# A new transition from the token stage to the attention groups in a one-core transformer block

## The reference, cut to what matters

```python
Q, K, V = heads(xn @ wq.T + bq), heads(xn @ wk.T + bk), heads(xn @ wv.T + bv)   # 16 heads of 32
Q, K = elu(Q) + 1, elu(K) + 1
KV    = einsum('bhsd,bhse->bhde', K, V)        # one 32x32 matrix per batch and head
K_sum = sum(K over tokens)
att   = (Q @ KV) / (Q @ K_sum + 1e-8)          # per token and head
attention = att @ wo.T + bo
# ffn: 8 experts' LoRA pairs (rank 8), the top 2 of a router, beside a shared LoRA pair
w = top2 weights of sigmoid(xn @ W_router) + bias
gate, up = (xn @ W + shared LoRA + weighted expert LoRA) for W in (W_gate, W_up)   # 1376 columns
ffn = (silu(gate) * up) @ W_down + shared LoRA + weighted expert LoRA
```

## Time and profile before

| | |
|---|---|
| median of 3 runs | 704.85 us |
| the profiled execution, its own time | 704.41 us |
| its span (first to last instruction) | 702.6 us |
| PE busy | 675.8 us (96%) |
| DVE busy | 388.3 us (55%) |
| ACT busy | 252.7 us (36%) |
| POOL busy | 125.3 us (18%) |
| mean granted TensorE clock | 0.992 |

### The profile page before, as it was taken

How to read it: one execution, slowest core, us unless ns; L and a number is a source line. 1 busy time by engine, 2 the same in 40 slices (tenths; PEclk the granted TensorE clock), 3 DMA queues, 4 the chain that set the end, 5 groups by cost and what they waited for, 6 DMA issues and landing times.

```text
span 702.6 us, 10690 instructions
## 1 busy us (share of the span) xinstructions
PE 675.8 (96%) x3636; PEld 553.8 (79%) x3636; DVE 388.3 (55%) x721; ACT 252.7 (36%) x401; POOL 125.3 (18%) x292
## 2 busy tenths in 40 slices
PE   6899999968999989999999999999999999999997
PEld 5888888856776767888888888888888888888886
DVE  5576676777678884444336534436544435544434
ACT  3343443553422532433324333224332324333322
POOL 3456655512623642000000000000000000000000
PEclk9999999999999999999999999999999999999999
DMA  7856668244655554100001600001600001300001
GB/s 231 298 186 211 198 210 293 92 151 161 240 215 204 210 180 160 79 0 0 0 8 53 240 0 0 0 0 61 239 0 0 0 0 60 119 0 0 0 0 60
DMA packets 23221, 73.03 MB, mean 104 GB/s; under 512 B 2768, under 2 KB 3408, under 8 KB 21152
## 3 DMA queue, kind: packets, MB, share of 16 engines
q1 hardware_dynamic: 22992, 72.45, 29.0%
q0 software_dynamic: 208, 0.30, 0.3%
HBM read 51.77 MB, written 20.97 MB: 104 GB/s over the span
## 4 chain that ended last, share of the span: by engine, by line
PE 64%; issue 14%; POOL 14%; DVE 3%; DMA 3%; POOLq 1%; ACT 1%; SPq 0%; DVEq 0%; ACTq 0%
PE bank L1369 17%; PE bank L1139 12%; PE bank L1140 12%; PE bank L1141 12%; PE bank L1344 6%; POOL x3r L600 2%; POOL qn_l L606 2%; PE bank L1357 1%; PE bank L1355 1%; DMA w_raw<-in_wvT 1%; POOL gt L556 1%; DMA x<-scr_x 1%; POOL vare L529 1%; POOL ssum L567 1%; POOL rstd L531 1%
## 5 line engine op out<-in xcount | busy, mean ns | idle before, releaser
L1139 PE MATMUL bank<-x,up_h 128*128 (+1 forms) x352 | 137.2, 390 | 1.4 <-DVE x3r L961 1.0
L1140 PE MATMUL bank<-x,up_h 128*128 (+1 forms) x352 | 137.2, 390 | 0.0
L1141 PE MATMUL bank<-x,up_l 128*128 (+1 forms) x352 | 137.1, 390 | 0.0
L1075 DVE TENSOR_TENSOR hf<-bank,silu 128x512 f32<-128x512 f32 x44 | 30.4, 691 | 155.9 <-issue 136.1
L1369 PE MATMUL bank<-dn,hid_h 128*128 128x512 f32 x352 | 108.9, 390 | 0.0
L1139 PEld LDWEIGHTS bank<-x,up_h 128*128 128x128 f32 x352 | 66.1, 188 | 18.2 <-issue 1.3
L618 ACT ACTIVATE hid_h<-hf 128x512 fp32r<-128x512 f32 x44 | 27.8, 632 | 142.3 <-DVE hf L1075 142.3
L1140 PEld LDWEIGHTS bank<-x,up_h 128*128 128x128 f32 x352 | 66.1, 188 | 14.1
L1141 PEld LDWEIGHTS bank<-x,up_l 128*128 128x128 f32 x352 | 66.1, 188 | 13.8
L1369 PEld LDWEIGHTS bank<-dn,hid_h 128*128 128x128 f32 x352 | 65.8, 188 | 13.8
L798 DVE TENSOR_TENSOR up_l<-up_raw,up_h 128x1024 fp32r<-128x1024 f32 x45 | 55.7, 1238 | 31.0 <-ACT up_h L618 31.0
(11 more groups left out here) (155 smaller groups left out, 1107.0 us busy)
## 6 DMA issues: line engine op xcount, KB each, us to landing
x<-scr_x SPq DMA_DIRECT2D x8, 2048.0 KB, 8.8
up_raw<-in_ffn_up SPq DMA_DIRECT2D x11, 768.0 KB, 5.9
scr_x<-xt SPq DMA_DIRECT2D x16, 512.0 KB, 5.6
xin<-in_x SPq DMA_DIRECT2D x16, 256.0 KB, 6.0
scr_z<-zt SPq DMA_DIRECT2D x16, 256.0 KB, 2.2
x3r<-in_x SPq DMA_DIRECT2D x16, 256.0 KB, 3.4
scr_att<-x3r SPq DMA_DIRECT2D x16, 256.0 KB, 2.0
z<-scr_z SPq DMA_DIRECT2D x4, 1024.0 KB, 4.8
```

The lines of the kernel that those rows point to most:

```text
L1075: nc.vector.tensor_tensor(hf[:], ps_u[:], silu[:], ALU.mult).then_inc(h_done, 1)
L1139: nc.tensor.matmul(dst, lh, rh, start=start, stop=False, **kw)
L1140: nc.tensor.matmul(dst, lh, rl, start=False, stop=False, **kw)
L1141: return nc.tensor.matmul(dst, ll, rh, start=False, stop=stop, **kw)
```

## The change: what it does

- **Tokens of group 0** get a buffer of their own (`x3a`), in the place of `up_raw`'s chunks 5 to 7. SP fills it during the token stage, one tile per pair of tiles (`x3a_load`), from what the stage has stored to `scr_x`. `x3` is loaded with group 1's tokens where group 0's were loaded before, and with group 2's and 3's after the queries of groups 1 and 2.
- **Query weights** `wq_h`, `wq_l` lie in the place of chunks 8 to 10 of `up_raw` and are split by ACT and DVE in tiles 8 to 11; `wo_h`, `wo_l` lie in chunks 2 to 4 and are split in tiles 12 to 15. DVE's subtraction for them stands behind the copy of `zraw`. Tiles 8 to 15 are written out, the loop covers tiles 2 to 7.
- **Loads**: only chunks 0 and 1 of `ffn_up` are loaded in the token stage; 5 to 7 behind group 0's queries, 2 to 4 behind `m_of`, 8 to 10 behind the last queries (`up_late_in`). Tile 15's `store_z` goes behind `x3r_load` 0 and 1.
- **The order** of all engines is new (below for PE): group 0's queries come directly behind `kv_transposed(0)`, group 1's queries fill the time of the denominators, `m_of(1)` comes later, and the 20 filler matmuls are gone.
- **ACT** makes the bias-and-max of the queries (a second `relu`), which DVE made before; `qf` is doubled (even and odd groups), `den` has a buffer of its own, `zst`, `zt`, `kvt` are moved.

```diff
-WO_PART = {TILES - KD + k: k for k in range(KD)}
+SPLIT_FROM = TILES - 2 * KD
+WQ_PART = {SPLIT_FROM + k: k for k in range(KD)}
+WO_PART = {SPLIT_FROM + KD + k: k for k in range(KD)}
+WO_CHUNK, X3_CHUNK, WQ_CHUNK = 2, 5, 8
...
+            def x3a_load(j):
+                for s in range(2):
+                    sp.wait_ge(scr_xd[s], 16 * (j + 1))
+                sp.dma_start(x3a[:, bass.ds(j, 1)]..., scr_x[:, bass.ds(j, 1)]).then_inc(x3a_in, 16)
...
-            with sp.Fori(0, TILES // 2 - 3) as p:
+            with sp.Fori(0, GT) as p:
                 stage1(2 * p + 2, 0)
                 store_z(2 * p)
-                load_up(p)
+                x3a_load(p)
                 load_dn(2 * p)
...
-            x3_load(0)
+            x3_load(1)
...
             sp.wait_ge(q_ready, KD)
-            x3_load(1)
+            for c in range(X3_CHUNK, WQ_CHUNK):
+                load_up(c)
             sp.wait_ge(bdn_done, 1)
-            for j in range(GT):
+            for j in range(2):
                 x3r_load(j, j)
+            store_z(TILES - 1)
+            sp.wait_ge(scr_zd, 16 * (TILES + 1))
+            for j in range(2, GT):
+                x3r_load(j, j)
+            sp.wait_ge(q_ready, KD * 2)
+            x3_load(2)
             sp.wait_ge(m_ready, BATCH * KD)
...
+            for c in range(WO_CHUNK, X3_CHUNK):
                 load_up(c)
...
             x4_load(0)
             z4_load(0)
+            for c in range(WQ_CHUNK, FC):
+                load_up(c, up_late_in)
...
+            residual(0, (0, 1))          # GpSimd
             normalised_lo(0)
-            residual(0)
+            residual(0, (2, 3))
...
+                    nc.scalar.activation(qf[g % 2][:, c, :], ps_q[c % 2][:], ACT.Relu, bias=bq_c[:, c:c + 1]
+                                         ).then_inc(qmax_done, 1)
...
+            kvt_hi(0)                    # ScalarE
+            act.wait_ge(kb_done, TILES)
...
             queries(0, (0,))
-            m_hi(0, (2, 3))
+            act.wait_ge(kf_done, TILES)
+            round_to(hrow[:], hrow_raw[:]).then_inc(hrow_done, 1)
+            queries(0, (1,))
             lora_out(TILES - 2)
             round_to(bdn[:], bdn_raw[:]).then_inc(bdnh_done, 1)
+            queries(0, (2, 3))
+            m_hi(0, range(KD))
             kvt_hi(1)
-            queries(0, (1,))
-            queries(0, (2, 3))
+            queries(1, (0,))
+            reciprocal_hi(0)
+            queries(1, (1,))
+            normalised_hi(0, range(KD))
             lora_out(TILES - 1)
+            queries(1, (2, 3))
             m_hi(1, range(KD))
...
+            compare(TILES - 1)           # VectorE
             kvt_lo(0)
+            lora_weighted(TILES - 2, TILES % 2)
+            select(TILES - 1)
+            queries(0, (0,))
             key_values(TILES - 1, TILES // 2 - 1)
             heads_of(1)
+            queries(0, (1,))
+            lora_weighted(TILES - 1, (TILES - 1) % 2)
             lora_lo(TILES - 2)
+            queries(0, (2,))
             dve.wait_ge(bdnh_done, 1)
             sub(bdn[0:ER, 1], bdn_raw[0:ER, 1], bdn[0:ER, 1]).then_inc(bdn_done, 1)
+            queries(0, (3,))
+            m_lo(0, (0, 1))
+            reciprocals(0)
+            m_lo(0, (2,))
             dve.wait_ge(bdn_done, 1)
+            reciprocal_lo(0)
+            m_lo(0, (3,))
+            scaled(0, (0, 1))
+            queries(1, (0,))
+            scaled(0, (2, 3))
+            queries(1, (1,))
+            kvt_lo(1)
             lora_lo(TILES - 1)
+            queries(1, (2, 3))
+            m_lo(1, range(KD))
+            group(1)
+            group(2)
...
+            kv_transposed(0)             # TensorE
+            queries(0, (0,))
+            keys_by_values(TILES - 1, TILES // 2 - 1, 1)
+            pe.wait_ge(kb_done, TILES)
+            queries(0, (1,))
+            lora_transposed(TILES - 2)
+            queries(0, (2,))
+            kv_transposed(1)
+            queries(0, (3,))
+            pe.wait_ge(vf_done, TILES)
+            pe.wait_ge(zraw_done, TILES)
+            pe.wait_ge(zt_done, TILES - 1)
+            m_of(0)
+            denominators(0)
+            queries(1, (0, 1))
+            pe.wait_ge(m_l_done, KD)
+            lora_transposed(TILES - 1)
+            pe.wait_ge(hrow_done, 1)
+            expand(0)
+            queries(1, (2, 3))
+            pe.wait_ge(qn_done, KD)
+            m_of(1)
+            pe.wait_ge(zt_done, TILES)
+            attention(0, (0,))
+            pe.wait_ge(m_l_done, BATCH * KD)
+            shared_down(1)
+            attention(0, (1,))
+            denominators(1)
+            attention(0, (2, 3))
+            expand(1)
+            queries(2, (0,))
+            group3(2)
```

More of the change, by code:

```diff
@@ L594, in _, with residual @@
             key_sums(1)
-            def residual(g):
-                for j in range(GT):
+            def residual(g, js=range(GT)):
+                for j in js:
                     pool.wait_ge(x3r_in[j], 16 * (g + 1))
@@ L990, in shared_down, with reciprocals @@
                     nc.vector.scalar_tensor_tensor(w, ps_sh[i][:], RSCALE, w, ALU.mult, ALU.add).then_inc(dnm_done, 1)
-            def group(g, first=False, last=False):
-                if not first:
+            def reciprocals(g):
+                dve.wait_ge(den_ready, g + 1)
+                nc.vector.tensor_scalar(den[:], ps_den[:], EPS, None, ALU.add).then_inc(dene_done, 1)
+                dve.wait_ge(dene_done, g + 1)
+                nc.vector.reciprocal(den[:], den[:]).then_inc(rden_done, 1)
@@ new lines, in reciprocal_lo, with scaled @@
+            def reciprocal_lo(g):
+                dve.wait_ge(rden_done, g + 1)
+                dve.wait_ge(rrh_done, g + 1)
+                nc.vector.scalar_tensor_tensor(rr[:], rr[:].bitcast(F32), lomask[:], den[:], ALU.mult, ALU.add
+                                               ).then_inc(rr_done, 1)
+            def scaled(g, cs):
+                for c in cs:
+                    dve.wait_ge(exp_ready, g * KD + c + 1)
+                    nc.vector.tensor_tensor(qf[g % 2][:, c, :], qf[g % 2][:, c, :], ps_exp[c][:], ALU.mult).then_inc(qn_done, 1)
@@ L994, in group @@
+            def group(g, last=False):
+                if g > 1:
                     queries(g, (1, 2, 3))
                     shared_down(g, FC - (GROUPS - 2) * SHG if last else SHG)
[L996 to L1002 removed]
@@ L1013, in group @@
+                if g == 1:
+                    shared_down(g)
+                if last:
+                    split_up_w(0, 0, 1).then_inc(upl_done, 1)
+                attention(g - 1, (1,))
+                reciprocals(g)
+                reciprocal_lo(g)
+                attention(g - 1, (2, 3))
                 if last:
                     split_up_b(0, 0).then_inc(upb_done, 1)
-                def scaled(c):
-                    dve.wait_ge(exp_ready, g * KD + c + 1)
-                    nc.vector.tensor_tensor(qf[:, c, :], qf[:, c, :], ps_exp[c][:], ALU.mult).then_inc(qn_done, 1)
@@ L1019, in group @@
-                for c in range(KD):
-                    if c == 2 and first:
-                        m_lo(1, (2, 3))
-                    if c == 3 and not last:
-                        queries(g + 1, (0,))
-                    scaled(c)
+                scaled(g, (0, 1, 2))
+                if not last:
+                    queries(g + 1, (0,))
+                scaled(g, (3,))
+            compare(TILES - 1)
             kvt_lo(0)
+            lora_weighted(TILES - 2, TILES % 2)
+            select(TILES - 1)
```

226 lines of the change are left out of this document (94 added, 132 removed).

## The result

The changed kernel takes 683.73 us, the median of 4 runs (683.19 to 686.11), beside 704.42 us for the kernel before in 4 runs. The ratio is 0.9737, with a 95% interval of 0.9712 to 0.9762. The forecast was 687.7 us with a range of 685.0 to 696.0. By the ratio the change gained 2.6% where 2.4% were forecast, and 0.9737 x 704.85 = 686.3 us lies in the range; the median itself lies 1.3 us under its lower end. In the profiled pair the total hides two misses that partly cancel: the transition gave 14.1 us where 15.8 were forecast, and the token stage 4.2 where 1.3 were.

The account below looks back on a forecast made before the run. PE's work was taken to bound the groups and PE's waiting the transition. The transition was to give 15.8 us less, with the token stage 17.1: 704.41 to 687.3, plus 0.4 for the median, 687.7 us; range 685.0 to 696.0.

Parts of the forecast that it names:

- PE's list sets the transition: From first `kv_transposed(0)` matmul to `denominators(1)`: PE's work plus remaining waits, 40.1 us instead of 55.9.
- The floor of 38.1: PE's work in us at full clock between `kv_transposed(0)` and `denominators(1)` in the new order, without waits.
- The covers: Behind `kv_transposed(0)`: PE's query chunks hide late inputs; first queries cost 0 (bounds 0 to 1.5), ACT's list 0 (0 to 1).
- rival 2: Before `denominators(1)`: DVE's list, not PE's, sets the pace, four pieces each 1 to 2 us late, 693.5 us; chance 0.20.
- The reciprocal: Between `denominators(1)`'s like in group 0 and `expand(0)`: PE fills 5.7 of 6.8 us; wait 1.0 us, bounds 0 and 2.5.
- POOL against DVE: In the transition: DVE's query adds and reciprocal low part slow down while POOL works; 1.0 us, bounds 0 and 2.5.
- Rival 1: In the new order the clock falls, fillers being gone: 1.1 us per fall, 691 us in all; chance 0.12.
- End of the groups: 2.36 MB of `ffn_up` go ahead of group 2's stores; cost 0, bounds 0 and 3; as rival 690.7 us, chance 0.07.
- SyncE's queue: x3_load(2), queued behind the last `store_z`, lands at 181.1 for PE's need at 186.2: cost 0, 5 us of slack.
- Token stage: Before `kv_transposed(0)`: smaller loads and the burst at tile 12 losing its `ffn_up` chunk, -1.3 us, bounds -2.0 and +1.0.
- The gap: At tile 12 of the token stage: its store lands late in a burst of loads; PE waited 1.17 us there.
- Rival 4: In the token stage: `x3a_load` waiting for just-issued stores blocks SyncE, 26 us longer, 713.7 us; chance 0.03.

Follow-up runs that it names:

- three edits: Changed kernel with residual adds behind the low parts, `m_lo(0, 3)` ahead of the reciprocal's low part, and ACT's reciprocal rounding ahead of an exp: 0.9732, 684.1 us.
- `ffn_up` earlier: Changed kernel with its two token-stage chunks of `ffn_up` moved two tiles earlier, to where the kernel before issued one: 0.9736, 684.2 us.

## Why the prediction was right, point by point

- **PE's list sets the transition.** Right. Work, one wait and the contention: 38.1 + 1.0 + 1.0 = 40.1 us were worked out, and the transition is 39.6 in three traces that have the changed order of the transition and 41.9 in the profiled one. The floor of 38.1 nearly holds: 39.6 less the wait of 1.17 is 38.4. That the total comes within 0.5 us is in part luck, since in the three traces the contention of the forecast costs nothing and the wait and the pieces of work are 0.5 us more than worked out.
- **The covers.** None of those taken as 0 failed: of the edges between `kv_transposed(0)` and `expand(0)` none shows in PE's waits. `heads_of(1)`, called the thinnest, was done at 143.6 (its last instruction from 142.88, 0.69 us) for 145.32, 1.7 us ahead instead of 0.3, 1.0 of it because DVE waited 0.73 us for the rank and not 1.75. The thinnest was another, the last query add of group 0 before `denominators(0)`, for which the prediction's own times leave 0.2 us (155.2 and 155.4): DVE ended it at 151.31, PE began at 151.46. DVE had waited 1.75 us for ACT's exp ahead of it, so ACT's list was within some 0.15 us of setting the pace there, and rival 2 was closer than the list of waits shows.
- **The reciprocal.** 1.0 us was forecast, 1.17 is the usual wait, and its releaser is `m_lo(0, 3)` as said.
- **POOL against DVE.** 1.0 us was taken, the slower instruction is there, but it hits a place that counts in the first trace only (0.77 us). VectorE's query adds read 0.69 to 1.60 us and cost PE nothing in the given order. What was not foreseen is that its price depends on when two residual loads land, so it comes and goes between executions. The Trainium skill (GPSIMD Engine Reference, Key points) says that VectorE instructions with two SBUF inputs contend with GpSimd; the 1.52 against 0.75 us of one and the same instruction agree with it.
- **Clock.** Rival 1 came true once, in the profiled execution, behind the wait of 1.94 us. It cost 41.9 - 39.6 - 0.77 = 1.5 us (the last number is the longer wait), where 1.1 were worked out. The second trace of the same kernel has no such stretch, all its 2 us rows from 150 to 168 us read 1.00, and so the forecast, which left the clock out of its sum, fits that one and not the profiled one. The sum for rival 2, 687.7 + 6, is 693.7 and not 693.5, and nothing in the prediction says why its range ends at 696.0 when its upper ends add up to 700.5.
- **End of the groups, SyncE's queue.** Right: 506.7 us behind `denominators(1)` in both kernels, and x3_load(2), issued at 169.15, was in time.
- **Token stage.** This is the step that was off in size: -1.3 us forecast, bounds -2.0 and +1.0; two traces against two give -3.2, the profiled pair -4.2, both outside the bounds. Of the 4.2, 2.3 stand at tiles 2 and 3, which took 9.92 and 9.59 us in the profiled execution of before and 9.21 and 7.99 in the changed one, in code that is the same; the second trace of before has 9.16 and 7.99. With one trace in hand I put that stretch into neither sum nor range. The gap (1.4 us) was named, and it goes; but its cause was said to be a burst at one place, and the experiment with the loads at that place shows no gap. What is shown is that without the stage's `ffn_up` loads the kernel before gains 3.7 us, with the interval at 2.0 to 5.3. The prediction counted one pass of the loop less for 0.2 us; PE, ACT and DVE have two less. Their ends take 0.5 us less in the profiled pair, and the kernel before with exactly these two written out is 0.26% faster, 1.8 us (interval 0.4 to 3.2), but not in its stage, so what they are worth is not shown. Rival 4 did not come: from tile 4 on no tile of the changed kernel's stage takes more than 7.99 us.

So the total came out near because the transition, by far the larger term, was worked from PE's own list. It lay at the low edge of the range because the token stage gives 3.2 us on average and not 1.3. That the profiled pair fits (18.3 us for 17.1) is luck in part: 2.3 us at tiles 2 and 3 that belong to that one execution of the kernel before stand against a fall of the clock and a longer wait, 2.3 us, that belong to that one of the changed kernel. The second traces give 15.9 us for the transition, 2.2 for the stage and -1.0 ahead of the first product, 17.1 in all.

## What to carry to other kernels

Where one engine's list is the bound in a stretch, write down its work between two marks that both orders share, and add only the waits that remain; the other engines' lists enter as arrival times, and a cover of 0.15 us held here. A transfer that is waited for behind others in its queue is worth as much as an order of instructions: issue the one that somebody waits for before the one that nobody needs yet (2 MB of weights ahead of one store cost this kernel some 2 us). And take a second trace of the kernel before, ahead of any sum over a stage: what differs between two traces of one kernel belongs into the range.

## What the hardware showed that I had not expected

- The same 128x512 VectorE instruction with two SBUF inputs took 0.75 or 1.52 us in two executions of one kernel; GpSimd's adds began 0.6 us behind its start in the one and 0.3 us before it in the other.
- The granted clock fell behind single PE waits of 1.94 us (the changed kernel), 2.02 (the kernel before, 0.91 from 20 to 40 us), 2.03 (bias-and-max on VectorE), 2.05 (tiles written out), 2.2 (three edits, 0.91 from 20 to 40 us) and 2.8 (`ffn_up` earlier, 0.93), and not behind those of 1.0 to 1.6 us before `expand(0)` and at 33 to 36 us. But it did not fall behind one of 2.5 either, at 36 us in the kernel with the bias on VectorE, where 20 to 40 us reads 1.00. The length of the wait alone does not decide it.
- A store of 512 KB issued behind 2 MB of loads in SyncE's queue freed its buffer 33.19 - 21.94 = 11.3 us after its issue; issued ahead of them, it had freed it when ACT asked, 8.2 us after. Nothing waited for the 2 MB of weights moved for this; they are first read at 78 us.
